# A linear attention layer in four overlapping passes: DMA order, three score banks, wider masks, and a norm placed behind the feature chain

## The chip, the cores and the metric

The kernel runs on one core of one Trainium2 chip. The metric is the device time of one execution in microseconds, lower is better. It is given as the median of several executions. One further execution was taken by the hardware profiler, and every row below is from that one.

The engines are PE (TensorE, matmuls; its weight loads are listed as PEld), DVE (VectorE), ACT (ScalarE), POOL (GpSimd) and SP (SyncE, which here only issues DMAs). Each runs its own instructions strictly in order; they meet only at semaphores.

## The reference, cut to what matters

The kernel computes two layers on 4 sequences of 512 tokens with 512 values each. A layer is half a feed-forward step, an attention, and half a feed-forward step again. The change lies in the first layer's attention, and in what is woven around it:

```python
x = x + 0.5 * _L0_ffn_ref(_layernorm(x), ...)        # routed splines, first half
x = x + _L0_attn_ref(_layernorm(x), ...)             # the attention below
x = x + 0.5 * _L0_ffn_ref(_layernorm(x), ...)        # routed splines, second half
# in _L0_attn_ref, with h = _layernorm(x):
def _softmax_kernel(x, R):
    n = sqrt(sum(x * x, -1));  x = x / maximum(n, 1e-06)
    p = einsum('...d,ed->...e', x, R)
    return concatenate([sin(p), cos(p)], -1) / sqrt(F)
q = rotary(h @ Wq.T + bq);  k = rotary(h @ Wk.T + bk)   # 16 query heads, 8 key heads
qp = _softmax_kernel(q, rand_matrix);  kp = _softmax_kernel(k, rand_matrix)
kv  = einsum('bhsf,bhsd->bsfd', kp, v)               # per token, over the heads
out = einsum('bhsf,bsfd->bhsd', qp, kv)
return out @ Wo.T + bo
```

The two sums run per token and over its heads, so no token sees another. The kernel puts 16 tokens side by side in one matmul (a group), computes all their scores, and multiplies by a mask that keeps each token's own.

## The kernel before, in words

**Passes.** The tokens come in four chunks of 512 (NCH = 4). `bass_macaron` calls `b_tensor`, `b_scalar`, `b_pool`, `b_sync` and `b_vector` for i = -1 to 3. Pass i works on four chunks at once (`b_roles`): the scores and outputs of chunk `now` = i; the projections and features of `new` = i + 1; the end of the first feed-forward half and the layer norm of `look` = i + 2; and the token routing of `back` = i - 1 for the second half. Chunks that do not exist are left out: pass -1 has no scores, passes 2 and 3 have no `look`, pass 3 has no `new`.

**Loop.** Each pass has a loop over y = 0 to 16. A pair y is two groups, 32 tokens. On PE `score(y)` makes the scores of a pair in a PSUM bank (L1310). On DVE `mask(y)` multiplies them by the constant mask into `sm` (L1688), which has two buffers. On PE `weighted(y)` multiplies by the values (L1323) into a bank of sums. After four pairs `sums(g)` reads that bank, on ACT (L1479), then on DVE (L1696). Between these stand the other chunks' steps at set values of y: twelve matmuls of 512 columns each for a projection (`project`, L1195, at y in QK_AT), its rotation on DVE (L1706) and POOL (L1595, L1599), the lengths (`length`, L1342), the values (`value`), and on DVE the routing steps (`route_pick_vector`, L517 and L519; `token_sums_vector`, L372 to L377; `route_ends_vector`, L527 to L539) and the look steps (`look_slope_vector` at y = 8; `scale_tiles_vector` at y = 12).

**Feature chain.** At y = 16 and behind the loop the lengths are spread (PE L1362, copied by ACT L1495) and six features follow (z = 0 and 1 of the keys, 2 to 5 of the two query pairs). Each is made by DVE (`angle`, L1730 to L1735), ACT (`feature`, L1501 and L1504, the high part) and DVE again (`low`, L1742, the low part). `ang` has two buffers, so feature z + 2 starts behind `low(z)`.

**Through DRAM.** The features are laid out anew by a trip through `feat_dram`. SP stores the high parts as they come and loads them back in another layout (`b_sync`), POOL does so with the low parts (`b_low_spread`). A load waits until the stores that it reads have landed. ACT copies the keys into `ksg` (`keys(g)`, L1512). `score(0)` of the next pass waits for all query loads, for `keys(0)`, and for `residual(3)`, which is the last step of this pass.

**End of a pass.** `output(u)` (L1195, twelve matmuls each for u = 0 to 3) makes the rows and `residual(u)` (L1750 on DVE) adds them to x. Two banks serve the four, so `output(2)` waits for `residual(0)` and `output(3)` for `residual(1)`. `residual(0)` stands behind `low(5)` on DVE. POOL then adds the bias (L1615). The layer norm of `look` takes the sums on DVE (L2108), two activations on ACT, `norm_refine_vector` on DVE, four activations that write the rows (L2150), sixteen transposes on PE, four for each column block (`next_turn_tensor`, L1933), and a split by ACT (L1941) and DVE (L1948). In passes 1 and 2 PE also runs the route steps (L447 to L479) of `back` before the next pass.

Of the kernel before, what the change touches and what calls it, by code (L numbers as in the profile page):

```python
# [1211 lines left out]
SCORE_BANK = (0, 1)  # L1212
SUM_BANK = (4, 5)
# [15 lines left out]
LOOK_SCALE, LOOK_NORM = 12, 16  # L1229
# [61 lines left out]
def b_tensor(k, pe, i):  # L1291
# [7 lines left out]
    def score(y):  # L1299
# [7 lines left out]
        need(pe, s["b_mask"], PAIRS * now + y - 1)  # L1307
        for q in range(2):
            toks = slice((2 * y + q) * GROUP, (2 * y + q + 1) * GROUP)
            ins = pe.matmul(k.ps[:, SCORE_BANK[y % 2], 256 * q:256 * q + 256].rearrange("p (h t) -> p h t", h=16),  # L1310
                            k.ksg[0:96, 2 * y + q, :], k.qs[0:96, :, toks], start=True, stop=True)
        ins.then_inc(s["b_s"], 1)

    def weighted(y):
        if y == 0:
            pe.wait_ge(s["b_vr"], 128 * (now + 1))
        if y % 4 == 0 and y >= 8:
            pe.wait_ge(s["b_ot_lo"], TPC * now + y // 4 - 1)
        pe.wait_ge(s["b_mask"], PAIRS * now + y + 1)
        for q in range(2):  # L1320
            g = 2 * y + q
            for j in range(4):
                ins = pe.matmul(k.ps[32 * j:32 * j + 32, SUM_BANK[y // 4 % 2], :]  # L1323
# [32 lines left out]
    def spread(a):  # L1356
        if a == 0:
            pe.wait_ge(s["b_r"], new + 1)
            if now is not None:
                pe.wait_ge(s["b_ot_lo"], TPC * now + 3)  # L1360
# [67 lines left out]
    if look is not None:  # L1428
# [42 lines left out]
def b_scalar(k, e, i):  # L1471
# [78 lines left out]
    ahead = look is not None and now is not None  # L1550
    if ahead:
        norm_root_scalar(k, e, look)
# [5 lines left out]
    if ahead:  # L1558
        next_rows(range(2))
    spread(2)  # L1560
    feature(2)
    if ahead:
        next_rows(range(2, TPC))
# [3 lines left out]
    if ahead:  # L1567
        next_turns(range(2))
    elif look is not None:
# [63 lines left out]
def b_low_spread(k, e, i):  # L1633
# [3 lines left out]
    for a in range(3):  # L1637
        for z in (2 * a, 2 * a + 1):
            e.wait_ge(s["b_f_lo"], 6 * i + z + 1)
            b_store(k, e, 1, z, s["b_lo_out"])  # L1640
        if a == 0:
            if i == 0:
                e.wait_ge(s["ug_out"], 16 * NCH)
            need(e, s["b_ksg"], 4 * i)
        if a == 1:
            need(e, s["b_s"], PAIRS * i)
        e.wait_ge(s["b_lo_out"], 96 * i + 32 * (a + 1))
        b_load(k, e, 1, a, 1 if a else 2, s["b_qs2" if a else "b_ks2"])


def b_sync(k, sp, i):
# [14 lines left out]
    for a in range(3):  # L1666
        for z in (2 * a, 2 * a + 1):
            sp.wait_ge(s["b_f_hi"], 6 * i + z + 1)
            b_store(k, sp, 0, z, s["b_hi_out"])
        if a == 0:  # L1670
            need(sp, s["b_ksg"], 4 * i)
        if a == 1:
            need(sp, s["b_s"], PAIRS * i)
        sp.wait_ge(s["b_hi_out"], 96 * i + 32 * (a + 1))
        for rows in ((0, 2) if a else (0, 1)):
            b_load(k, sp, 0, a, rows, s["b_qs" if a else "b_ks"])


def b_vector(k, V, i):
# [4 lines left out]
    def mask(y):  # L1684
        e.wait_ge(s["b_s"], PAIRS * now + y + 1)
        need(e, s["b_pv"], PAIRS * now + y - 1)
        for q in range(2):
            ins = e.tensor_tensor(k.sm[:, y % 2, q], k.ps[:, SCORE_BANK[y % 2], 256 * q:256 * q + 256]  # L1688
                                  .rearrange("p (h t) -> p h t", h=16), bcast(k.c["same"].unsqueeze(1), [P, 16, 16]),
                                  ALU.mult)  # L1690
        ins.then_inc(s["b_mask"], 1)

    def sums(g):
        e.wait_ge(s["b_ot_hi"], TPC * now + g + 1)
        out = grouped(k.ot_lo)[:, :, :, 8 * g:8 * g + 8]
        e.scalar_tensor_tensor(out=out, in0=k.ps[:, SUM_BANK[g % 2], :].rearrange("p (a h g) -> p a h g", g=8, a=4),  # L1696
# [73 lines left out]
    for y in range(PAIRS + 1):  # L1770
# [16 lines left out]
        if look is not None:  # L1787
# [14 lines left out]
            if y == LOOK_NORM and now is not None:  # L1802
# [1216 lines left out]
```

## Time and profile before

| what | value |
|---|---|
| median of 3 runs | 2215.35 us (2211.72 to 2221.18) |
| the profiled execution's own time | 2216.09 us |
| its span | 2214.3 us |
| PE busy | 1947.4 us, 88% of the span |
| DVE busy | 1254.1 us, 57% |
| ACT busy | 716.2 us, 32% |
| POOL busy | 275.5 us, 12% |

The span is the time between the first and the last instruction in the trace. An engine's busy time leaves out its waits. Below, times are microseconds from the start of the span. The passes with scores are found by the first `score(0)` of each: 311.45, 399.06, 493.16 and 578.61 us; the last outputs start at 620.57 us.

### The profile page before, as it was taken

The page shows a single profiled execution, that of the slowest core. Times are in us where ns is not written, and L with a number is a line of the kernel's source. Part 1 is how long each engine was busy: PE and PEld are TensorE (multiplying, and loading weights), DVE is VectorE, ACT ScalarE, POOL GpSimd, SP SyncE. Part 2 cuts the span into 40 slices and gives each one's busy share as a digit, 9 for nine tenths or more (in the row PEclk, how much of TensorE's full clock was granted, in tenths as well). Part 3 has the DMA queues.
Part 4 walks back from the last instruction along what each step waited for, and adds up shares of the span by engine and source line. Part 5 has one row for each costly group of instructions (what it writes and reads, how often), then busy time and mean ns, then how long its engine had stood idle before and what let it go on. Part 6 is the DMA issues. An engine that isn't in the chain of part 4 may idle for free.

```text
span 2214.3 us, 28789 instructions
## 1 busy us (share of the span) xinstructions
PE 1947.4 (88%) x11782; PEld 925.7 (42%) x11782; DVE 1254.1 (57%) x2297; ACT 716.2 (32%) x1105; POOL 275.5 (12%) x224
## 2 busy tenths in 40 slices
PE   3876768878655999899999999999999999999999
PEld 2443324434333444344444444444444444444444
DVE  4677568677765564636673456636663456533332
ACT  3553143253422123222352234422352234311211
POOL 1840234332100000000000100010000100000000
PEclk9987778979767999999999999999999999999999
DMA  7223242141323213211021111111021111132321
GB/s 242 93 84 88 110 91 56 36 91 18 74 77 115 96 64 117 95 67 40 28 77 40 65 48 58 48 58 44 25 77 36 70 48 58 48 114 100 120 98 64
DMA packets 92457, 164.93 MB, mean 74 GB/s; under 512 B 44134, under 2 KB 55718, under 8 KB 87718
## 3 DMA queue, kind: packets, MB, share of 16 engines
q1 hardware_dynamic: 89446, 156.79, 22.3%
q0 software_dynamic: 2880, 6.31, 1.1%
q8 instruction: 93, 1.52, 0.3%
q14 instruction: 38, 0.31, 0.0%
HBM read 137.89 MB, written 25.17 MB: 74 GB/s over the span
## 4 chain that ended last, share of the span: by engine, by line
PE 50%; DVE 4%; ACT 2%; issue 1%; ACTq 0%; DVEq 0%
PE ps L1195 27%; PE ps L2018 12%; PE ps L2532 2%; PE ps L2551 1%; DVE arena L2696 1%; PE ps L2528 1%; PE ps L2534 1%; PE ps L2478 1%; PE ps L2569 1%; PE ps L2553 1%; PE ps L2555 1%; PE ps L2560 1%; PE ps L2558 1%; PE ps L2475 1%; DVE arena L2073 0%
## 5 line engine op out<-in xcount | busy, mean ns | idle before, releaser
L1195 PE MATMUL ps<-arena 128*128 128x512 f16 (+1 forms) x4512 | 1015.6, 380 | 25.1 <-DVE arena L2073 12.9
L1195 PEld LDWEIGHTS ps<-arena 128*128 128x128 f16 x4512 | 433.2, 98 | 539.2 <-issue 42.4
L2018 PE MATMUL ps<-arena 128*128 128x512 f16 x1536 | 343.8, 379 | 12.5 <-DVE arena L2101 9.3
L2018 PEld LDWEIGHTS ps<-arena 128*128 128x128 f16 x1536 | 146.6, 97 | 185.8 <-DVE arena L2101 12.1
L2073 DVE SCALAR_TENSOR_TENSOR arena<-arena,ps 128x512 f32<-128x512 f32 x128 | 87.9, 687 | 208.4 <-ACT arena L2040 207.8
L2040 ACT ACTIVATE arena<-ps,arena 128x512 f32<-128x512 f32 x128 | 87.6, 684 | 358.7 <-PE ps L1195 358.5
L2625 ACT ACTIVATE arena<-ps 128x1024 f32<-128x1024 f32 (+3 forms) x128 | 90.1, 704 | 254.7 <-PE ps L2534 254.5
L2730 DVE CAST arena<-arena 128x1024 f16<-128x1024 f32 (+3 forms) x128 | 66.2, 517 | 150.3 <-ACT arena L2625 148.3
L2696 DVE TENSOR_REDUCE arena<-ps 128x2 f32<-128x256 f32 (+3 forms) x128 | 99.6, 820 | 65.0 <-PE ps L2478 65.0
L2101 DVE SCALAR_TENSOR_TENSOR arena<-ps,arena 128x512 f32<-128x512 f32 x64 | 44.0, 688 | 134.5 <-PE ps L2018 134.3
L2082 DVE SCALAR_TENSOR_TENSOR arena<-ps,arena 128x512 f32<-128x512 f32 x128 | 95.8, 748 | 39.5 <-PE ps L1195 39.1
L2676 POOL TENSOR_TENSOR arena<-arena 128x512 f16<-128x512 f32 x32 | 37.1, 1158 | 624.7 <-ACT arena L2603 624.7
L2732 DVE TENSOR_TENSOR arena<-arena 128x1024 f16<-128x1024 f32 (+3 forms) x128 | 111.4, 870 | 4.4
L2064 DVE TENSOR_TENSOR arena<-arena 128x512 f16<-128x512 f32 x128 | 90.9, 710 | 4.0 <-ACT arena L2032 4.0
L1933 PE MATMUL ps<-arena 128*128 128x128 f32 x192 | 32.9, 323 | 67.2 <-ACT arena L2150 64.7
L2680 POOL TENSOR_TENSOR arena<-arena 128x512 f32<-128x512 f32 x16 | 19.0, 1187 | 581.7 <-DVE arena L2743 581.7
L2032 ACT ACTIVATE arena<-arena 128x512 f16<-128x512 f32 x128 | 79.7, 622 | 17.5 <-DVE arena L2082 17.5
L741 PE MATMUL ps<-arena 128*128 128x128 f32 x240 | 46.9, 341 | 37.6 <-DVE arena L979 17.6
L2600 ACT ACTIVATE arena<-ps 128x512 f32<-128x512 f32 x32 | 19.1, 597 | 166.7 <-PE ps L1195 166.7
L2532 PE MATMUL ps<-arena 32*128 32x512 f16 (+3 forms) x768 | 72.9, 293 | 0.0
L1688 DVE TENSOR_TENSOR arena<-ps,arena 128x256 f32<-128x256 f32 x128 | 47.6, 417 | 41.8 <-PE ps L1310 41.1
L1323 PE MATMUL ps<-arena 128*32 128x64 f32 x1024 | 41.8, 292 | 26.3 <-DVE arena L1688 26.2
(269 smaller groups left out, 2356.6 us busy)
## 6 DMA issues: line engine op xcount, KB each, us to landing
arena<-wug_dram SPq DMA_DIRECT2D x128, 512.0 KB, 3.3
arena<-wd_hi_dram SPq DMA_DIRECT2D x16, 1024.0 KB, 5.0
arena<-wd_lo_dram SPq DMA_DIRECT2D x16, 1024.0 KB, 7.1
wug_dram<-arena SPq DMA_DIRECT2D x4, 2048.0 KB, 16.5
arena<-feat_dram SPq DMA_DIRECT2D x24, 256.0 KB, 3.9
arena<-_attn_hidden_states_dram SPq DMA_DIRECT2D x4, 1024.0 KB, 16.9
arena<-in_L_ffn_W_up_dram SPq DMA_DIRECT2D x8, 512.0 KB
arena<-in_L_ffn_W_down_dram SPq DMA_DIRECT2D x4, 1024.0 KB, 7.3
```

The costliest lines, as they stand in the source:

```text
L1195: ins = pe.matmul(out, left[a](c), right[b](c), start=(at == 0), stop=(at == 3 * n - 1))
L2018: ins = pe.matmul(k.ps[:, bank, :], act[x][:, slot, cols], wd[y][:, f, :], start=(f == 0 and m == 0), stop=(f == 7 and m == 2))
L2032: e.activation(k.act_hi[:, g % ACT_SLOTS, :], k.prod[:, g % 2, :], ACT.Copy).then_inc(s["f_hi"], 1)
L2040: e.activation(k.th[:, g % 2, :], k.ps[:, GATE_BANK, :], ACT.Tanh, scale=k.wscale[:, FB + a:FB + a + 1])\
L2064: e.tensor_tensor(k.act_lo[:, g % ACT_SLOTS, :], k.prod[:, g % 2, :], k.act_hi[:, g % ACT_SLOTS, :], ALU.subtract)\
L2073: e.scalar_tensor_tensor(out=th, in0=th, scalar=1.0, in1=k.ps[:, GATE_BANK, :], op0=ALU.add, op1=ALU.mult)\
L2082: e.scalar_tensor_tensor(out=k.prod[:, g % 2, :], in0=k.ps[:, UP_HALF_BANK, :], scalar=k.wscale[:, a:a + 1], in1=th, op0=ALU.mult, op1=ALU ...
L2532: pe.matmul(k.ps[:, bank, queries], x[rows, 4 + b, keys], y[rows, b, queries], start=False, stop=False)
L2625: e.activation(k.p32[:, t % 2, :, queries], k.ps[:, 0:2, queries], ACT.Exp, scale=SCORE).then_inc(s["c_exp"], 1)
L2696: e.tensor_reduce(k.mx[:, u, 4 * b + 2 * j:4 * b + 2 * j + 2], k.ps[:, bank:bank + 2, 0:(u + 1) * P], AXX, ALU.max).then_inc(s["c_max"], 1)
L2730: e.tensor_copy(k.p_hi[:, t % 2, :, queries], k.p32[:, t % 2, :, queries]).then_inc(s["c_p_hi"], 1)
L2732: e.tensor_tensor(k.p_lo[:, t % 2, :, queries], k.p32[:, t % 2, :, queries], k.p_hi[:, t % 2, :, queries], ALU.subtract).then_inc(s["c_p_l ...
```

## The change

There are three edits in one.

1. Features. Both queues store the four query features (z = 2 to 5) first, wait once for all, and then load both query pairs. Before, the first pair was loaded ahead of the second pair's stores.
2. Scores. `SCORE_BANK` has three banks instead of two and `SUM_BANK` one instead of two. PE issues `score(y + 1)` at loop step y, ahead of `weighted(y - 1)`, so scores run one more pair ahead. With one bank of sums, `weighted(4)`, `weighted(8)` and `weighted(12)` wait until DVE has read the sums of the four pairs before. A mask is one DVE instruction of 512 columns instead of two of 256.
3. Norm of `look`. Where a pass has both `now` and `look` (passes 0 and 1), its sums, roots and rows move from the end of the loop and from between the features to behind `low(5)` and `residual(0)`. On PE the four transposes move behind `output(2)`. On ACT they come ahead of `keys(0)`, as before.

```diff
-SCORE_BANK = (0, 1)
-SUM_BANK = (4, 5)
+SCORE_BANK = (0, 1, 4)
+SUM_BANK = 5
...
 def b_tensor(k, pe, i):
...
-        need(pe, s["b_mask"], PAIRS * now + y - 1)
+        need(pe, s["b_mask"], PAIRS * now + y - 2)
...
-        if y % 4 == 0 and y >= 8:
-            pe.wait_ge(s["b_ot_lo"], TPC * now + y // 4 - 1)
+        if y % 4 == 0 and y:
+            pe.wait_ge(s["b_ot_lo"], TPC * now + y // 4)
...
-            if y < PAIRS:
-                score(y)
-            elif new is not None:
+            if y == 0:
+                score(0)
+            if y + 1 < PAIRS:
+                score(y + 1)
+            if y == PAIRS and new is not None:
                 spread(0)
...
-        next_turn_tensor(k, pe, look, 0)
-        next_turn_tensor(k, pe, look, 1)
     output(0)
     output(1)
+    output(2)
     if look is not None:
-        next_turn_tensor(k, pe, look, 2)
-        next_turn_tensor(k, pe, look, 3)
-    output(2)
+        for c in range(KC):
+            next_turn_tensor(k, pe, look, c)
...
 def b_vector(k, V, i):
...
-        for q in range(2):
-            ins = e.tensor_tensor(k.sm[:, y % 2, q], k.ps[:, SCORE_BANK[y % 2], 256 * q:256 * q + 256]
-                                  .rearrange("p (h t) -> p h t", h=16), bcast(k.c["same"].unsqueeze(1), [P, 16, 16]),
-                                  ALU.mult)
+        ins = e.tensor_tensor(k.sm[:, y % 2].rearrange("p q h t -> p (q h) t"),
+                              k.ps[:, SCORE_BANK[y % 3], :].rearrange("p (h t) -> p h t", t=16),
+                              bcast(k.c["same"].unsqueeze(1), [P, 32, 16]), ALU.mult)
...
-            if y == LOOK_NORM and now is not None:
-                next_sums()
...
-    if look is not None and now is not None:
-        norm_refine_vector(k, V, look)
...
-    if look is not None and now is None:
+    residual(0)
+    if look is not None:
         next_sums()
         norm_refine_vector(k, V, look)
-    residual(0)
-    turned(0)
     residual(1)
-    turned(1)
-    turned(2)
-    turned(3)
     residual(2)
+    for c in range(KC):
+        turned(c)
     residual(3)
```

The queue of SP is the first place. These are its DMAs of one chunk: the values out and in, then the features out (`feat_dram<-arena`) and in. Before:

```order
L1659 DMA values_dram<-arena 128x4x256
L1663 DMA arena<-values_dram 16x32x32 x8
L1622 DMA feat_dram<-arena 8x16x512 x2
L1629 DMA arena<-feat_dram 32x8x512 x2
L1622 DMA feat_dram<-arena 8x16x512 x2
L1629 DMA arena<-feat_dram 32x8x512 x2
L1622 DMA feat_dram<-arena 8x16x512 x2
L1629 DMA arena<-feat_dram 32x8x512 x2
```

and of the change:

```order
L1653 DMA values_dram<-arena 128x4x256
L1657 DMA arena<-values_dram 16x32x32 x8
L1613 DMA feat_dram<-arena 8x16x512 x2
L1620 DMA arena<-feat_dram 32x8x512 x2
L1613 DMA feat_dram<-arena 8x16x512 x4
L1620 DMA arena<-feat_dram 32x8x512 x4
```

The last pair's two stores have moved past the first pair's two loads. (Lines of the change are lower by three to nine numbers, as its file is shorter.)

The second place is PE from the last steps of pass 0 to the first of pass 1. L1362 is `spread`, L1352 `turned`, L1933 (L1924) the transposes of the next rows, L1195 the outputs and then a projection. Before:

```order
L1362 MATMUL ps<-arena 128x512
L1352 MATMUL ps<-arena 128x512 x2
L1362 MATMUL ps<-arena 128x512
L1933 MATMUL ps<-arena 128x128 x8
L1195 MATMUL ps<-arena 128x512 x24
L1933 MATMUL ps<-arena 128x128 x8
L1195 MATMUL ps<-arena 128x512 x24
L1310 MATMUL ps<-arena 128x256 x2
L1195 MATMUL ps<-arena 128x512 x12
L1310 MATMUL ps<-arena 128x256 x2
L1323 MATMUL ps<-arena 32x64 x8
```

and of the change:

```order
L1362 MATMUL ps<-arena 128x512
L1352 MATMUL ps<-arena 128x512 x2
L1362 MATMUL ps<-arena 128x512
L1195 MATMUL ps<-arena 128x512 x36
L1924 MATMUL ps<-arena 128x128 x16
L1195 MATMUL ps<-arena 128x512 x12
L1310 MATMUL ps<-arena 128x256 x4
L1195 MATMUL ps<-arena 128x512 x12
L1310 MATMUL ps<-arena 128x256 x2
L1323 MATMUL ps<-arena 32x64 x8
```

Three outputs now stand ahead of all sixteen transposes and one behind them, and two pairs of scores ahead of the first projection.

The third place is DVE at the end of pass 0 in the change, from `low(3)` on. L2099 to L2109 are the sums of the next rows (before they were L2108 to L2118, ahead of `angle(0)`), L1747 is `residual`, L1939 the split of the transposed rows:

```order
L1739 SCALAR_TENSOR_TENSOR arena<-arena 128x512 x2
L1747 SCALAR_TENSOR_TENSOR arena<-ps,arena 128x512
L2099 BN_STATS arena<-arena 128x6 x4
L2107 BN_AGGR arena<-arena 128x2 x4
L2109 TENSOR_SCALAR arena<-arena 128x4
L2127 TENSOR_TENSOR arena<-arena 128x4
L2128 SCALAR_TENSOR_TENSOR arena<-arena 128x4
L2129 SCALAR_TENSOR_TENSOR arena<-arena 128x4
L2130 TENSOR_SCALAR arena<-arena 128x4
L2131 SCALAR_TENSOR_TENSOR arena<-arena 128x4
L1747 SCALAR_TENSOR_TENSOR arena<-ps,arena 128x512 x2
L1939 TENSOR_TENSOR arena<-ps,arena 128x512 x4
```

`residual(1)` and `residual(2)` now stand behind the norm, and `residual(3)` behind all four splits.

## Rows read from the trace of the kernel before

**Rows 1.** Windows: length; busy PE, PEld, DVE, ACT, POOL; PE clock, DMA share, GB/s.

```profile
579.00:620.00 41.00, 22.99 (x335) 13.44 (x333) 33.19 (x83) 9.52 (x17) 0.00 (x0) 0.62 0.01 2
...
694.00:2214.00 1520.00, 1471.60 (x8709) 666.95 (x8707) 780.22 (x1299) 464.23 (x723) 75.70 (x64) 1.00 0.20 67
```

**Rows 2.** Waits of PE from 311 to 621: us in total, times, longest.

```profile
PE ps L1323 <- DVE arena L1688: 26.2, 13, 4.2
```

**Rows 3.** Timeline: masks and weighted sums, passes 1 and 2; start, duration, instruction [idle before].

```profile
413.85 0.65 PE L1323 MATMUL ps<-arena 128*32 128x64 f32 x16 [1.56 <-DVE arena L1688]
414.44 2.77 PE L1195 MATMUL ps<-arena 128*128 128x512 f16 x12
...
498.90 0.76 DVE L1688 TENSOR_TENSOR arena<-ps,arena 128x256 f32<-128x256 f32 x2 [4.34 <-PE ps L1310]
...
510.69 0.65 PE L1323 MATMUL ps<-arena 128*32 128x64 f32 x16 [3.71 <-DVE arena L1688]
511.27 4.45 PE L1195 MATMUL ps<-arena 128*128 128x512 f16 x12
```

**Rows 4.** Timeline: PE and DVE around the sums of pass 0.

```profile
344.63 0.65 PE L1323 MATMUL ps<-arena 128*32 128x64 f32 x16
...
346.17 0.69 DVE L1696 SCALAR_TENSOR_TENSOR arena<-ps,arena 128x512 f16<-128x512 f32 x1
...
360.89 0.66 PE L1323 MATMUL ps<-arena 128*32 128x64 f32 x16 [2.84 <-DVE arena L1688]
```

**Rows 5.** Timeline: last query loads of pass 0 and first scores of pass 1.

```profile
395.41 0.60 POOL L1629 DMA_DIRECT2D arena<-feat_dram  x1 [4.66 <-DMA feat_dram<-arena]
...
399.06 0.41 PE L1310 MATMUL ps<-arena 96*128 96x256 f16 x2 [2.68 <-issue]
399.28 4.44 PE L1195 MATMUL ps<-arena 128*128 128x512 f16 x12
```

**Rows 6.** Timeline: the norm of pass -1, which has no scores.

```profile
299.12 2.87 DVE L2108 BATCH_NORM_STATS2 arena<-arena 128x6 f32<-128x512 f32 x4
...
307.19 1.94 PE L1933 MATMUL ps<-arena 128*128 128x128 f32 x8 [16.34 <-ACT arena L2150]
309.69 1.97 PE L1933 MATMUL ps<-arena 128*128 128x128 f32 x8 [0.56 <-DVE arena L1948]
```

**Rows 7.** Timeline: start and end of the feature chains in passes 0, 1 and 2.

```profile
368.95 0.60 ACT L1495 ACTIVATE arena<-ps 128x512 f32<-128x512 f32 x1 [10.17 <-PE ps L1362]
...
384.82 0.69 DVE L1742 SCALAR_TENSOR_TENSOR arena<-arena 128x512 f16<-128x512 f32 x1 [0.85 <-ACT arena L1504]
...
457.10 0.60 ACT L1495 ACTIVATE arena<-ps 128x512 f32<-128x512 f32 x1 [9.91 <-PE ps L1362]
...
473.20 0.69 DVE L1742 SCALAR_TENSOR_TENSOR arena<-arena 128x512 f16<-128x512 f32 x1 [0.85 <-ACT arena L1504]
...
548.64 0.69 DVE L1730 SCALAR_TENSOR_TENSOR arena<-ps,arena 128x512 f32<-128x512 f32 x1 [3.47 <-ACT arena L1495]
...
562.10 0.69 DVE L1742 SCALAR_TENSOR_TENSOR arena<-arena 128x512 f16<-128x512 f32 x1 [0.85 <-ACT arena L1504]
```

**Rows 8.** Timeline of PE: from the route steps of pass 1 to pass 2.

```profile
482.19 1.04 PE L447 MATMUL ps<-arena 128*128 128x128 f32 x8
483.06 2.75 PE L1195 MATMUL ps<-arena 128*128 128x512 f16 x12
...
493.16 0.61 PE L1310 MATMUL ps<-arena 96*128 96x256 f16 x2
```

**Rows 9.** Timeline: the end of pass 2 and two waits of pass 3.

```profile
574.28 4.22 POOL L1615 TENSOR_TENSOR arena<-arena 128x512 f32<-128x512 f32 x4
575.62 3.45 DVE L517 TENSOR_TENSOR arena<-arena 128x512 f32<-128x512 f32 x1
...
580.09 0.68 DVE L517 TENSOR_TENSOR arena<-arena 128x512 f32<-128x512 f32 x1
...
612.67 0.76 DVE L1688 TENSOR_TENSOR arena<-ps,arena 128x256 f32<-128x256 f32 x2 [1.26 <-PE ps L1310]
```

More of the change, by code:

```diff
@@ L1228 @@
 LOOK_START, LOOK_PLACE, LOOK_SLOPE, LOOK_VALUE = 3, 6, 8, 11
-LOOK_SCALE, LOOK_NORM = 12, 16
+LOOK_SCALE = 12
 def need(eng, sem, value):
@@ L1359, in spread @@
             if now is not None:
-                pe.wait_ge(s["b_ot_lo"], TPC * now + 3)
+                pe.wait_ge(s["b_mask"], PAIRS * (now + 1))
         need(pe, s["b_spread"], 3 * new + a)
@@ L1548, in next_turns @@
             turn_scalar(k, e, look, c, NEXT_TURN[c])
-    ahead = look is not None and now is not None
-    if ahead:
-        norm_root_scalar(k, e, look)
     if now is None:
@@ L1557, in b_scalar @@
     feature(1)
-    if ahead:
-        next_rows(range(2))
     spread(2)
     feature(2)
-    if ahead:
-        next_rows(range(2, TPC))
     feature(3)
@@ L1566, in b_scalar @@
     feature(5)
-    if ahead:
-        next_turns(range(2))
-    elif look is not None:
+    if look is not None:
         use_log(e)
@@ L1636, in b_low_spread @@
     need(e, s["b_qs2"], 32 * i)
[L1637 to L1648, printed above, removed]
+    for z in range(2):
+        e.wait_ge(s["b_f_lo"], 6 * i + z + 1)
+        b_store(k, e, 1, z, s["b_lo_out"])
+    if i == 0:
+        e.wait_ge(s["ug_out"], 16 * NCH)
+    need(e, s["b_ksg"], 4 * i)
+    e.wait_ge(s["b_lo_out"], 96 * i + 32)
+    b_load(k, e, 1, 0, 2, s["b_ks2"])
+    for z in range(2, 6):
+        e.wait_ge(s["b_f_lo"], 6 * i + z + 1)
+        b_store(k, e, 1, z, s["b_lo_out"])
+    need(e, s["b_s"], PAIRS * i)
+    e.wait_ge(s["b_lo_out"], 96 * i + 96)
+    for a in (1, 2):
+        b_load(k, e, 1, a, 1, s["b_qs2"])
 def b_sync(k, sp, i):
@@ L1665, in b_sync @@
     need(sp, s["b_qs"], 64 * i)
[L1666 to L1676, printed above, removed]
+    for z in range(2):
+        sp.wait_ge(s["b_f_hi"], 6 * i + z + 1)
+        b_store(k, sp, 0, z, s["b_hi_out"])
+    need(sp, s["b_ksg"], 4 * i)
+    sp.wait_ge(s["b_hi_out"], 96 * i + 32)
+    for rows in (0, 1):
+        b_load(k, sp, 0, 0, rows, s["b_ks"])
+    for z in range(2, 6):
+        sp.wait_ge(s["b_f_hi"], 6 * i + z + 1)
+        b_store(k, sp, 0, z, s["b_hi_out"])
+    need(sp, s["b_s"], PAIRS * i)
+    sp.wait_ge(s["b_hi_out"], 96 * i + 96)
+    for a in (1, 2):
+        for rows in (0, 2):
+            b_load(k, sp, 0, a, rows, s["b_qs"])
 def b_vector(k, V, i):
@@ L1695, in sums @@
         out = grouped(k.ot_lo)[:, :, :, 8 * g:8 * g + 8]
-        e.scalar_tensor_tensor(out=out, in0=k.ps[:, SUM_BANK[g % 2], :].rearrange("p (a h g) -> p a h g", g=8, a=4),
+        e.scalar_tensor_tensor(out=out, in0=k.ps[:, SUM_BANK, :].rearrange("p (a h g) -> p a h g", g=8, a=4),
                                scalar=O_SCALE, in1=grouped(k.ot_hi)[:, :, :, 8 * g:8 * g + 8],
@@ L1841, in b_vector @@
     low(5)
-    if look is not None and now is None:
+    residual(0)
+    if look is not None:
         next_sums()
         norm_refine_vector(k, V, look)
-    residual(0)
-    turned(0)
     residual(1)
-    turned(1)
-    turned(2)
-    turned(3)
     residual(2)
+    for c in range(KC):
+        turned(c)
     residual(3)
```

6 lines of the change are left out of this document (3 added, 3 removed).

## The prediction, made before the changed kernel ran

> **What bounds the kernel now.** I read the windows first. From 694 us on PE is busy for 1471.6 of 1520 us at full clock [rows 1]; the change touches none of that, it only moves it in time. So what counts is when the four passes end. In pass 3 PE works 23.0 us of 41 and DVE 33.2 us [rows 1]: there DVE sets the pace. In passes 0 to 2 PE is mostly busy but stands at joints. The waits of PE name the largest: 26.2 us in 13 waits of the weighted sums for a mask [rows 2]. That looks like the prize for a third score bank, so I asked of each wait what DVE did before it. In pass 2 it first stood 4.34 us without scores and was late afterwards [rows 3]. In pass 0, before the wait of 2.84 us at 360.89 [rows 4], it worked through the look steps: there more scores help little.
>
> The second joint is the start of a pass. `score(0)` of pass 1 waits 2.68 us after the outputs; POOL's last query load was issued at 395.41 [rows 5]. So the trip through DRAM is the bound there. At the start of pass 2 PE comes straight from its route steps [rows 8], and the loads are hidden.
>
> **The change, part by part.** All shifts are against the time before; minus is earlier.
>
> *Stores ahead of loads.* It takes a load's time out of the way of POOL's last stores, worth 2.68 us at 399.06 at most, and nothing at the other starts. Whether it pays depends on what else is late then, which is the norm, next.
>
> *The norm behind the features.* Take pass 2 as the price of a feature chain without the norm: 548.64 to 562.79 (562.10 + 0.69), 14.15 us [rows 7]. In pass 0 the copy that the chain waits for ends at 369.55; I put it 0.3 us later (below) and add 0.1 for the hop: `low(5)` ends at 369.95 + 14.15 = 384.1, before at 385.51 [rows 7]. That is the gain, 1.4 us. What now hangs behind it is in pass -1, where the norm also stands behind the features: from the first sum at 299.12 to the end of the last transpose at 311.66 (309.69 + 1.97), 12.54 us [rows 6]. Then come `output(3)` and `residual(3)`, which must be done before `score(0)`:
>
> 384.1 + 0.69 (`residual(0)`) + 12.54 = 397.3 for the last transpose; + 4.44 for twelve matmuls at the low clock, since PE has idled (as at 399.28 after 2.68 us [rows 5]) = 401.8; + 0.8 for `residual(3)` and its hop = 402.6.
>
> Before it was 399.06 [rows 5]: 3.5 us later, and by then the loads, which were in by 399.06 before and now go out earlier, have landed. Part comes back: `project(0)` follows PE's own work and runs its twelve in 2.77 as at 414.44 [rows 3] instead of 4.44 (-1.7), while one more pair of scores stands ahead of it (+0.3). First joint: **+2.1 us**.
>
> Second joint, in times of pass 1 before. The copy ends at 457.70 [rows 7]; with the loop's -1.1 (below) `low(5)` ends at 457.7 - 1.1 + 0.1 + 14.15 = 470.85, before at 473.89. Then + 0.69 + 12.54 = 484.1 for the last transpose. The route steps wait for its split too. That takes 1.5 us: the second row of transposes began at 309.69, and its split block was ready at about 308.2, half of the first row [rows 6]. So the route steps start at 485.6 instead of 482.19, +3.4. `output(3)` before took 2.75 [rows 8]; PE has now idled for several us ahead of the transposes, so I take 4.44, +1.7. Behind it the chain to 493.16 is as it was. Second joint: **+5.1 us**, the gain of the chain included.
>
> *Scores ahead, three banks.* In pass 2 DVE's idle 4.34 us before 498.90 now take in that mask and the first route pick, some 2.4 us (mask 0.7, pick 1.7: the tensor op and its reduction, of which the first is 0.68 elsewhere); the extra pair on PE costs 0.3. The mask that PE waits for at 510.69 [rows 3] comes 2.1 us earlier, and that shift runs down DVE's and POOL's chain to the end of the pass. PE alone could gain more, as a wait of 1.56 us left the next twelve at 2.77 and one of 3.71 at 4.45 [rows 3], but the next wait for sums eats it. Pass 2: **-2.1 us**.
>
> *One bank of sums.* `weighted(8)` ran at 344.63 and must now wait for the sums of the first half, which DVE finished at 346.86 (346.17 + 0.69) [rows 4]: 2.3 us on PE. DVE is not earlier there, because its look step waits for a PE step that does not move. Of this, most is slack: PE later waited 2.84 us for the mask at 360.89 [rows 4], and that wait shrinks. The look step that sets it is itself some 0.3 us later. So pass 0 ends +0.3. In pass 1 the same chain gains since two masks no longer stand ahead of look steps, waiting for scores: -1.1 at the copy. Both numbers are already in the two joints.
>
> *Wide masks.* Two of 256 columns take 0.76 [rows 3]; one instruction of 512 columns out of PSUM takes 0.69 [rows 4]. 64 masks save 4.5 us of DVE, on its path only in the DVE-bound half of pass 3, six to nine masks: 0.4 us. The Trainium skill (VectorE: DVE Perf Modes, the section on the TRN2 errata) puts a PSUM-source instruction at 120 cycles plus one per column; by its figure at 0.96 GHz two of 256 would be 0.78 us and one of 512 0.66, an estimate that would make the saving 0.12 instead of 0.07 and the term 0.7. The trace has both times, so they stand.
>
> *Pass 3.* At 575.62 a DVE multiply that takes 0.68 took 3.45, while POOL's bias adds ran (574.28 to 578.50) [rows 9]. POOL stood in its queue behind the last loads. With the stores ahead it is spared one such round; in pass 0 POOL's wait for landed stores took 4.66 us [rows 5]. The adds then end at about 573.8, before 575.62. So -2.77, and DVE is busy without a gap from there to the first mask and on. Later a mask waited 1.26 us for scores [rows 9] that are now there. With the masks: **-4.4 us**. The Trainium skill (SBUF — State Buffer, Who interferes with whom) says that a DVE instruction with two SBUF inputs contends with a GpSimd instruction that reads SBUF. By it the 3.45 is contention and goes with the overlap; the row agrees.
>
> **Sum.** +2.1 + 5.1 - 2.1 - 4.4 = +0.7 us. Against the profiled execution's 2216.09 that is 2216.8; the median before is 0.7 below that execution, so I forecast **2216 us**: no change that could be told. A measurement of this kernel tells about 0.5%, 11 us, from no change.
>
> **Bounds.** Down: `output(3)` at the full clock at both joints (-3.4), pass 2 also keeps PE's faster projection (-1.7), pass 3 saves all its later waits (-1): -5.4 in sum. Up: pass 2 gains nothing (+2.1); POOL still overlaps and pass 3 gains 1.6 only (+2.8); the wait for sums of 2.3 us stays on the path in passes 0 and 1 (+4.6): +10.2 in sum. That is 2210 to 2226.
>
> **Rivals.**
>
> *It does what it says* (0.12): the mask waits go, and the norm hides behind the loads. For it: 26.2 us of waits [rows 2], 2.68 us at the loads [rows 5]. Against it: in passes 0 and 1 DVE was at work before its late masks, and the norm's 12.5 us are longer than the trip of the last pair. With both joints at zero instead of +7.2, the 2.7 us gained, and half of the 26.2, of which 3.4 are counted already (2.1 in pass 2, 1.3 in pass 3): 0.7 - 7.2 - 2.7 - 13.1 + 3.4 = -18.9, about 2197.
>
> *The bank of sums decides* (0.08), the other side. Three groups in each of four passes now make PE wait for ACT and DVE: 12 waits. One was worked out at 2.3 us [rows 4]. If no later slack takes them in, since each also costs PE its clock, they are 12 x 2.3 = 28 us, and the time 2240. From about 0.9 us a wait kept on the path it passes 11 us and decides. Against it: ahead of `weighted(4)` PE has a projection of 2.77 us to run in passes 0 to 2, longer than the two reads of a bank by ACT and DVE (0.69 on DVE [rows 4], about as much on ACT), and DVE's pace, not PE's, sets pass 3.
>
> *The clock.* PE's granted clock in pass 3 was 0.62 [rows 1], a mix of its two levels, 1.2 and 2.4 GHz; the low one cost 1.7 us for twelve matmuls after one wait of 3.71 us and nothing after one of 1.56 [rows 3]. If the new waits fall so that PE drops once more in each of the four passes, that is +6.8 us, still no change by the bound. Its chance, 0.1, is part of the forecast's 0.80. The Trainium skill (TensorE: Matmul & The Clock Gate, HAM oscillation) says that waits between bursts throttle PE again; the two rows agree.
>
> **How the numbers follow.** Forecast 0.80, between 2210 and 2226 but for a run's scatter of 4 us; 0.12 for the faster rival, 0.08 for the slower. So faster by over 0.5% 0.12, within 0.80, slower 0.08. The range is the forecast's own with that scatter downwards: 2207 to 2225. The rivals lie outside it.
>
> **What would show it.** Of each step: `score(0)` of pass 1 some 3.5 us after where it was, with `output(3)` and not a load before it, and the loads landed; between the first transposes and the end of `residual(0)` some 8 us on PE with little work. In pass 1 the route steps 15 us behind `low(5)` or more. A wait of `weighted(8)` for the sums of about 2.3 us in pass 0, and a shorter one than 2.84 at the thirteenth mask. L517 at 0.68 throughout in pass 3, POOL's adds done by then. A mask in one instruction of 0.69. The forecast is wrong if the transposes start less than 7 us behind `residual(0)`, if the passes' first halves shift by more than 2 us, or if anything behind 694 us changes its length.

## The result, and the profile after

The changed kernel takes 2218.86 us (median of 20 runs, 2214.70 to 2226.37), the kernel before 2214.25 us in the same comparison: ratio 1.0026, 95% interval 1.0017 to 1.0036. That is 4.6 us more, within the 0.5% that I called no change, and 2.9 us above the forecast. The profiled execution has a span of 2218.1 us.

First the waits of PE from 311 to 626 us (total, times, longest), against [rows 2]:

```profile
PE ps L1323 <- DVE arena L1693: 14.4, 7, 3.4
PE ps L1195 <- DVE arena L1747: 10.4, 3, 4.6
PE ps L1323 <- DVE arena L1685: 9.4, 7, 4.1
```

The waits for masks (L1685) fell from 26.2 to 9.4 us. In their place stand seven waits for the sums (L1693) of the one bank, 14.4 us, and outputs now wait 10.4 us for residuals, where before one waited 4.6 us. PE's timeline shows the two waits for sums in pass 0, and then the two joints, against [rows 4], [rows 5] and [rows 8]:

```profile
347.31 0.65 PE L1323 MATMUL ps<-arena 128*32 128x64 f32 x16 [2.08 <-DVE arena L1693]
...
362.45 0.65 PE L1323 MATMUL ps<-arena 128*32 128x64 f32 x16 [1.94 <-DVE arena L1693]
...
385.64 4.45 PE L1195 MATMUL ps<-arena 128*128 128x512 f16 x12 [3.74 <-DVE arena L1747]
393.47 1.97 PE L1924 MATMUL ps<-arena 128*128 128x128 f32 x8 [3.38 <-ACT arena L2141]
395.99 1.97 PE L1924 MATMUL ps<-arena 128*128 128x128 f32 x8 [0.56 <-DVE arena L1939]
397.76 3.62 PE L1195 MATMUL ps<-arena 128*128 128x512 f16 x12
402.16 0.61 PE L1310 MATMUL ps<-arena 96*128 96x256 f16 x4 [0.79 <-DVE arena L1747]
402.61 2.76 PE L1195 MATMUL ps<-arena 128*128 128x512 f16 x12
...
487.34 1.97 PE L447 MATMUL ps<-arena 128*128 128x128 f32 x8 [1.41 <-DVE arena L1939]
489.10 4.02 PE L1195 MATMUL ps<-arena 128*128 128x512 f16 x12
...
500.50 1.04 PE L1310 MATMUL ps<-arena 96*128 96x256 f16 x4
```

The reader is to see the chain of the norm in the second half of pass 0: residual(0), transposes at 393.47, `output(3)`, `residual(3)`, `score(0)` at 402.16. What I had not foreseen is on POOL. Its timeline in pass 0, and the end of pass 2, against [rows 9]:

```profile
381.26 0.61 POOL L1620 DMA_DIRECT2D arena<-feat_dram  x1 [2.75 <-DMA feat_dram<-arena]
381.86 1.19 POOL L1613 DMA_DIRECT2D feat_dram<-arena  x2
386.29 0.60 POOL L1613 DMA_DIRECT2D feat_dram<-arena  x1 [3.24 <-issue]
390.55 0.61 POOL L1613 DMA_DIRECT2D feat_dram<-arena  x1 [3.66 <-issue]
396.88 1.19 POOL L1620 DMA_DIRECT2D arena<-feat_dram  x2 [5.72 <-DMA feat_dram<-arena]
...
578.69 1.19 POOL L1620 DMA_DIRECT2D arena<-feat_dram  x2 [5.01 <-DMA feat_dram<-arena]
579.89 4.24 POOL L1606 TENSOR_TENSOR arena<-arena 128x512 f32<-128x512 f32 x4
```

and DVE's multiply there, then one wide mask:

```profile
581.45 3.24 DVE L517 TENSOR_TENSOR arena<-arena 128x512 f32<-128x512 f32 x1
...
507.42 0.68 DVE L1685 TENSOR_TENSOR arena<-ps,arena 128x512 f32<-128x512 f32 x1
```

The third and fourth query store wait 3.24 and 3.66 us "for issue". Of the first, 0.4 us is the wait for its own low part (ready at 383.44); nothing in the program holds the rest. The last low part was ready at 384.98 (384.29 + 0.69), its store went out at 390.55. So POOL's loads left at 396.88, later than the 395.41 of [rows 5], and the adds still ran beside L517, which took 3.24 us, against 3.45 before. SP, with the same order, issued its four stores from 381.28 to 384.85; only the fourth stood back, by 1.2 us, as its high part was ready at 384.25.

To compare executions, which differ by some us before the first pass, I count from POOL's first feature store in pass -1 (at 289.57 us before, 289.40 after). All in us, each line from the one profiled execution of its kernel; "rest" runs from the start of the last outputs to the end of the span:

| kernel | first store to pass 0 | pass 0 | pass 1 | pass 2 | pass 3 | rest |
|---|---|---|---|---|---|---|
| before | 21.9 | 87.6 | 94.1 | 85.5 | 42.0 | 1593.7 |
| changed | 23.6 | 89.2 | 98.3 | 84.1 | 40.9 | 1592.6 |
| changed, again | 24.1 | 89.6 | 97.5 | 83.7 | 40.6 | 1592.8 |
| edit 1 alone | 24.6 | 88.7 | 94.0 | 85.9 | 44.0 | 1598.5 |
| edit 2 alone | 22.7 | 87.4 | 91.8 | 82.8 | 41.1 | 1599.5 |
| edit 3 alone | 22.6 | 89.8 | 98.8 | 85.1 | 43.2 | 1592.7 |
| without edit 1 | 21.9 | 90.5 | 95.6 | 83.6 | 40.7 | 1592.6 |
| without edit 2 | 24.8 | 87.4 | 98.7 | 85.2 | 44.1 | 1598.8 |
| without edit 3 | 24.3 | 91.8 | 94.3 | 84.3 | 40.4 | 1593.3 |
| changed, low parts by SP | 23.1 | 89.2 | 96.0 | 82.3 | 40.3 | 1593.9 |
| changed, adds first | 24.3 | 89.6 | 98.3 | 84.0 | 39.7 | 1593.8 |
| before, low parts by SP | 21.9 | 87.9 | 93.6 | 85.3 | 38.8 | 1593.9 |
| edit 2, low parts by SP | 22.1 | 88.9 | 92.4 | 84.3 | 39.7 | 1593.8 |

### The profile page after: what moved, and what is told of

Same layout as the page of the kernel before. It is cut to its first block, busy times and chain, and to the rows that moved or that the text cites. A ratio compares the mean times of both kernels' runs of the same rounds, so it can differ in the third digit from the quotient of the medians.

```text
span 2218.1 us, 28723 instructions
## 1 busy us (share of the span) xinstructions
PE 1951.7 (88%) x11782; PEld 927.4 (42%) x11782; DVE 1251.9 (56%) x2233; ACT 709.8 (32%) x1099; POOL 276.2 (12%) x224
## 4 chain that ended last, share of the span: by engine, by line
PE 50%; DVE 4%; ACT 2%; issue 1%; ACTq 0%; DVEq 0%
PE ps L1195 27%; PE ps L2009 12%; PE ps L2523 2%; PE ps L2542 1%; DVE arena L2687 1%; PE ps L2519 1%; PE ps L2525 1%; PE ps L2469 1%; PE ps L2560 1%; PE ps L2544 1%; PE ps L2546 1%; PE ps L2551 1%; PE ps L2549 1%; PE ps L2466 1%; DVE arena L2064 0%
## 5 line engine op out<-in xcount | busy, mean ns | idle before, releaser
L1195 PE MATMUL ps<-arena 128*128 128x512 f16 (+1 forms) x4512 | 1017.0, 380 | 30.1 <-DVE arena L2064 12.9
L1195 PEld LDWEIGHTS ps<-arena 128*128 128x128 f16 x4512 | 433.4, 98 | 546.9 <-issue 45.8
L2009 PE MATMUL ps<-arena 128*128 128x512 f16 x1536 | 343.8, 379 | 12.5 <-DVE arena L2092 9.3
L2064 DVE SCALAR_TENSOR_TENSOR arena<-arena,ps 128x512 f32<-128x512 f32 x128 | 87.9, 687 | 208.4 <-ACT arena L2031 207.8
L1924 PE MATMUL ps<-arena 128*128 128x128 f32 x192 | 34.4, 336 | 65.1 <-ACT arena L2141 63.4
L784 PE MATMUL ps<-arena 128*128 128x512 f16 x256 | 63.1, 390 | 0.9 <-DVE arena L979 0.9
L1323 PE MATMUL ps<-arena 128*32 128x64 f32 x1024 | 41.7, 293 | 23.9 <-DVE arena L1693 14.4
```

Source lines behind the costliest of these rows:

```text
L1195: ins = pe.matmul(out, left[a](c), right[b](c), start=(at == 0), stop=(at == 3 * n - 1))
L2009: ins = pe.matmul(k.ps[:, bank, :], act[x][:, slot, cols], wd[y][:, f, :], start=(f == 0 and m == 0), stop=(f == 7 and m == 2))
L2064: e.scalar_tensor_tensor(out=th, in0=th, scalar=1.0, in1=k.ps[:, GATE_BANK, :], op0=ALU.add, op1=ALU.mult)\
```

## The experiments

My theory after the result (A): the norm makes the two joints late, as predicted, and POOL's queue takes only a few transfers that have not landed, so edit 1 makes POOL's loads later instead of earlier. The rivals: the order of the DMAs hides behind the norm (B); the bank of sums makes the loss.

**The edits undone one at a time.** Edit 1 undone is the two functions `b_low_spread` and `b_sync` as before, edit 3 undone the removed lines of the diff put back. In short:

```diff
 # dma_order_back
+    for a in range(3):
+        for z in (2 * a, 2 * a + 1): ... b_store(k, e, 1, z, s["b_lo_out"])
+        ... b_load(k, e, 1, a, 1 if a else 2, s["b_qs2" if a else "b_ks2"])
 # norm_back
+            if y == LOOK_NORM and now is not None:
+                next_sums()
 # banks_back
-SCORE_BANK = (0, 1, 4)
-SUM_BANK = 5
+SCORE_BANK = (0, 1)
+SUM_BANK = (4, 5)
```

> The changed kernel with the DMA order of before in both queues (the first query pair is loaded ahead of the second pair's stores). Theory A, POOL's queue holds only two or three transfers, so that its third and fourth store wait to be issued: no store waits any more, the last POOL load of pass 0 goes out at about 395.4 + 1 instead of 396.88, score(0) of pass 0 comes 1.5 us earlier (311.5), the adds of pass 2 end before L517, which falls from 3.24 to 0.68, and pass 3 is 2.6 us shorter: in sum 3 to 4 us less than the changed kernel. Theory B, the order of the DMAs is hidden behind the norm: score(0) of passes 1 to 3 and the time stay within 1 us of the changed kernel. Both: the start of pass 1 is set by output(3) and stays at 402.

> The changed kernel with the norm of look in its old place. Theory A (the norm behind residual(0) is what makes the joints late, but POOL's late loads stand right behind it): pass 1 starts with a wait for POOL's loads at about 401.5 instead of 402.2, so the first joint gives back under 1 us; the second joint, where PE has the route steps, gives back 3 to 5 us, and the time falls by 3 to 5 us. Theory B, the prediction's joints as they stand (2.1 and 5.1): it falls by 7. If it does not fall at all, the lateness of the joints is from the sum bank instead.

> The changed kernel with edit 2 undone (two score banks, two banks of sums, narrow masks), so edits 1 and 3 alone. If these two make the loss, as theory A has it (the norm's place and POOL's full queue), it stays 4 to 7 us slower than before, and the start of pass 1 relative to the first feature store of pass -1 is again near 112.5. If the bank of sums made the loss, it is back at the time of before.

Without edit 1: 2215.26 against 2212.49 us before, ratio 1.0013 (0.9999 to 1.0027). No store waits for issue any more and pass 0 starts at 21.9 again, but the adds still ran beside L517, which took 3.02 us; that part of the expectation failed. Pass 1 starts where it did, counted from the first store (112.4 against 112.8), as both said. The loss of 2.8 us stands against 4.6 and 5.5 in the two comparisons of the changed kernel, so undoing edit 1 gives back 2 to 3 us, less than the 3 to 4 of A and more than the 1 of B.

Without edit 3: 2220.77 against 2212.49, 1.0024 (1.0010 to 1.0038). It did not fall. PE's waits say why: pass 1 now begins with a wait of 6.08 us for the loads, which POOL issued at 400.34 and 400.94. Partly the norm had hidden them: in the changed kernel the second load landed at 401.7, 0.4 us ahead of the end of `residual(3)`. Partly they are later: counted from the first store, the last low part is ready at 98.9 instead of 95.6, as the norm's steps stand among the features again, and the loads leave at 111.2 instead of 107.5. Edit 2 alone has that late end too (98.1 against 95.9 before). The expectation of 3 to 5 us gained failed for these reasons.

Without edit 2: 2227.89 against 2213.74, 1.0050 (1.0033 to 1.0066). So the bank of sums did not make the loss; without it the kernel is 8.6 us slower than the changed one in the same comparison (2219.28, next).

**Each edit alone, and the changed kernel again.**

> The kernel before with edit 1 alone (all query stores ahead of the query loads, in both queues). If POOL's full queue is what edit 1 costs (seen in the runs with and without it), POOL's last load of pass 0 goes out 1 to 3 us later than in the kernel before, the waits of score(0) at the starts of passes 0 and 1 grow, L517 stays long in pass 3, and it is 4 to 8 us slower than before. The prediction's account had it neutral to 2.7 us faster at the start of pass 1 and 2.77 faster in pass 3.

> The kernel before with edit 3 alone (the norm of the next rows behind residual(0)). The prediction's joints: +2.1 and +5.1, so 7 us slower than before, with output(3) and residual(3) ahead of score(0) of pass 1 and no wait for loads. From the two runs with edit 2 that differ in it alone (2212.7 without, 2215.3 with) it is 3 to 4 us.

> The kernel before with edit 2 alone: three score banks, one bank of sums, wide masks. The prediction's terms: pass 2 and pass 3 gain 2.1 and 1.7, passes 0 and 1 lose 0.3 and gain 1.1, so 3 to 4.5 us faster than before. Rival, the bank of sums decides: seven waits of 14.4 us in sum for the sums take the place of the mask waits (26.2 down to about 9) and the time is that of before or up to 3 us slower.

> The changed kernel itself once more, as the measure for the other runs of this call and for its own spread. Theory: the 2.4 us by which pass 1 was longer in its first profile than in the profiles of two kernels that do the same there (98.34 against 95.62 and 95.99) is the granted clock of one execution, not the change; then in this profile output(3) of pass 1 takes 2.75 instead of 4.02 and L447 1.09 instead of 1.97, or again the long times if it belongs to the kernel. Median 2216 to 2219.

Edit 1 alone costs most of all: 2226.35 against 2214.14, 1.0054 (1.0037 to 1.0071). POOL, PE and DVE in its timeline:

```profile
385.82 0.60 POOL L1622 DMA_DIRECT2D feat_dram<-arena  x1 [1.96 <-issue]
389.13 0.60 POOL L1622 DMA_DIRECT2D feat_dram<-arena  x1 [2.71 <-issue]
396.48 1.19 POOL L1629 DMA_DIRECT2D arena<-feat_dram  x2 [6.75 <-DMA feat_dram<-arena]
...
401.29 0.58 PE L1310 MATMUL ps<-arena 96*128 96x256 f16 x2 [6.04 <-issue]
...
577.51 4.59 DVE L517 TENSOR_TENSOR arena<-arena 128x512 f32<-128x512 f32 x1
```

The wait at the start of pass 1, which the edit was to remove (2.68 us in [rows 5]), is 6.04 us, and the multiply beside the adds went from 3.45 to 4.59. Of the 9.3 us by which this profile's span is longer, 4.8 lie in the rest.

Edit 3 alone: 2223.43 against 2214.14, 1.0039 (1.0025 to 1.0053). In the table pass 0 is 2.2 us longer and pass 1 4.7. These are not the prediction's 2.1 and 5.1, which are counted between other points: from first score to first score its terms for this edit make 3.2 (3.5 less 0.3 for the one bank) and 4.5 (5.1 - 1.7 for `project(0)` + 1.1 that edit 2 was to gain), 7.7 in sum for a measured 6.9. The first scores of pass 1 wait for `residual(3)`, not for a load:

```profile
403.54 0.38 PE L1310 MATMUL ps<-arena 96*128 96x256 f16 x2 [0.85 <-DVE arena L1739]
```

Edit 2 alone: 2212.71 against 2213.74, 0.9990 (0.9975 to 1.0006). In its profile the four passes take 6.0 us less than before (303.1 against 309.1), but the rest takes 5.7 us more. Two stretches that differ, 60 to 80 and 280 to 320 us behind the start of the last outputs; before, then edit 2 alone (columns as in [rows 1]; the clock is the third number from the end):

```profile
680.57:700.57 20.00, 10.54 (x48) 6.39 (x49) 8.40 (x21) 7.70 (x12) 0.00 (x0) 0.69 0.03 5
900.57:920.57 20.00, 15.36 (x67) 6.46 (x66) 16.85 (x23) 4.84 (x6) 0.00 (x0) 0.94 0.42 163
920.57:940.57 20.00, 18.55 (x84) 8.06 (x83) 13.84 (x25) 10.55 (x16) 0.00 (x0) 0.98 0.25 80
```

```profile
674.04:694.04 20.00, 9.60 (x36) 5.68 (x37) 8.58 (x20) 7.70 (x12) 0.00 (x0) 0.56 0.02 3
894.04:914.04 20.00, 15.82 (x73) 6.86 (x71) 15.86 (x22) 4.90 (x6) 0.00 (x0) 0.99 0.52 184
914.04:934.04 20.00, 18.10 (x70) 7.46 (x71) 14.06 (x26) 9.19 (x14) 0.00 (x0) 0.84 0.17 53
```

PE's clock was low for longer in both stretches. In the second stretch the two windows have to be taken together: 3.2 us of 40 at 1.2 GHz before and 6.8 with edit 2 alone, and 3.6 us more at half speed are 1.8 us of work at most. A third place lies 520 to 540 us behind the last outputs, with a granted share of 1.00 before and 0.91 now. The starts of the same DVE instructions in both traces, counted from the last outputs, show what each place costs: edit 2 alone is 0.9 us late already 20 us behind them (its last outputs took 13.41 us against 12.48), 2.6 behind the first place, 3.9 behind the second and 5.6 behind the third. So work that the change does not touch gave the gain back in this execution. Edit 1 alone and the kernel without edit 2 have a rest of 1598.5 and 1598.8 and lose at the same three places. Why these three kernels and not the others stays open; each has one profile, and the times of one kernel spread by up to 12 us (edit 2 alone: 2206.53 to 2218.37), so it is not shown that all their executions do so.

The changed kernel again: 2219.28 against 2213.74, 1.0018 (1.0004 to 1.0033). Pass 1 took 97.5 us, its `output(3)` 3.48 and its first route step L447 1.97; so my theory that the long pass 1 was one execution's clock holds only in part: 0.8 us of it. Where both ran at the full clock (1.09 and 2.75, without edit 1 and with the low parts by SP, below), pass 1 took 95.6 and 96.0. And in this second profile it was a load, not `residual(3)`, that pass 1 waited for:

```profile
403.47 0.60 PE L1310 MATMUL ps<-arena 96*128 96x256 f16 x4 [1.90 <-issue]
```

`residual(3)` was done at 402.29. POOL's fourth query store had waited 4.47 us, its second load left at 399.17 and landed 4.1 us later. So the full queue of edit 1 costs 1.2 us at this joint in one of two profiles of the changed kernel.

**The two costs of edit 1 by themselves.**

```diff
 # low_by_sp: in b_sync, and z = 4, 5 left out in b_low_spread
         b_store(k, sp, 0, z, s["b_hi_out"])
+        if z > 3:
+            sp.wait_ge(s["b_f_lo"], 6 * i + z + 1)
+            b_store(k, sp, 1, z, s["b_hi_out"])
 # low_by_sp: in b_low_spread, ahead of the two loads
+    e.wait_ge(s["b_hi_out"], 128 * i + 128)     # all of SP's stores
 # adds_first: in b_low_spread, pass 2 only
+    ahead()      # the four bias adds
     for a in (1, 2):
         b_load(k, e, 1, a, 1, s["b_qs2"])
 # small_ring
-dynamic_dma_scratch_size=1024
+dynamic_dma_scratch_size=512
```

> The changed kernel, but the low parts of the last two features are stored by SP's queue instead of POOL's. Theory A (POOL's queue is full): POOL's loads no longer follow two stalled stores, the last load of pass 0 goes out at about 391 instead of 396.9, score(0) of pass 0 at 310 to 311.5 instead of 313.0, L517 in pass 3 falls from 3.24 to 0.68: 3 to 5 us less in all. Rival (POOL's issue waits only mirror busy DMA engines): SP's stores of the low parts land as late, POOL's loads go out within 1 us of before, and the time is unchanged. The start of pass 1 stays at 401 to 402, set by the norm.

> The changed kernel, with POOL's four bias adds of pass 2 ahead of its last two query loads instead of behind. If contention of these adds with the DVE multiply L517 costs 2.6 us at the start of pass 3's second half, L517 takes 0.68 throughout and the last outputs start some 2.5 us earlier (623.0), while the loads go out at 578.7 as now. Rival: DVE has slack there, L517 gets short but the time stays (under 0.5 us).

> The changed kernel with the on-chip memory for the descriptors of POOL's DMAs halved, from 1024 to 512. Theory A (a POOL store waits to be issued because the descriptors of earlier transfers, not yet landed, fill this memory): the issue waits appear already at the second store or load and grow, POOL's loads go out several us later, and each start of a pass with them, 5 to 20 us in all. Rival (DVE's work keeps POOL from writing descriptors, or the DMA engines are full): the issue waits of 3 to 4 us at the third and fourth store stay as they are.

Low parts by SP: 2217.43 against 2212.49, 1.0020 (1.0006 to 1.0034). POOL's last loads left at 390.30 and 390.90, six us earlier, and L517 took 0.69; the profiled span fell by 4.6 us to 2213.5, but the medians show no gain: 4.9 us above the kernel before, where the changed kernel was 4.6 and 5.5. The start of pass 1 stayed with `residual(3)`.

Adds first: 2216.47 against 2212.49, 1.0011 (0.9997 to 1.0025). L517 took 0.69, and the first mask of pass 3 came 0.6 us behind the first scores (581.15, 581.79) instead of 2.8 (584.60, 587.41). But pass 3 is only 1.0 to 1.3 us shorter than in the two profiles of the changed kernel, not 2.5: the rest went to later waits, which I did not follow one by one.

Small ring: 2248.84 us (2 runs) against 2214.14, 1.0156 (1.0125 to 1.0187). POOL in its pass 0, and PE's first scores of pass 1:

```profile
388.72 0.61 POOL L1613 DMA_DIRECT2D feat_dram<-arena  x1 [3.78 <-DVE arena L1739]
392.84 0.60 POOL L1620 DMA_DIRECT2D arena<-feat_dram  x1 [3.51 <-DMA feat_dram<-arena]
396.89 0.60 POOL L1613 DMA_DIRECT2D feat_dram<-arena  x1 [3.45 <-issue]
401.21 0.60 POOL L1613 DMA_DIRECT2D feat_dram<-arena  x1 [3.71 <-issue]
...
411.90 0.61 POOL L1620 DMA_DIRECT2D arena<-feat_dram  x1 [2.89 <-DMA feat_dram<-arena]
415.42 0.60 POOL L1620 DMA_DIRECT2D arena<-feat_dram  x1 [2.91 <-issue]
...
419.17 1.01 PE L1310 MATMUL ps<-arena 96*128 96x256 f16 x4 [9.20 <-issue]
```

With half the memory for descriptors the waits begin at the second key store (388.72, its low part was ready at 386.02), and each later transfer goes out only when the one before it has landed, mostly some 0.3 us behind it. That costs about 30 us against the changed kernel, more than the 5 to 20 expected. DVE's work was not changed and the transfers were the same, so the rival falls and theory A stands, that this memory is what holds POOL. A larger memory was not tried.

**Versions that use it.**

```diff
 # before_lows_by_sp (norm, banks as before): SP as in low_by_sp, one mask of 512 columns; POOL:
+    b_load(k, e, 1, 1, 1, s["b_qs2"])           # behind the stores of z = 2, 3
+    e.wait_ge(s["b_hi_out"], 128 * i + 128)     # all of SP's stores
+    b_load(k, e, 1, 2, 1, s["b_qs2"])
 # lows_by_sp_and_banks: the same queues, and edit 2
```

> The kernel before with two edits: SP's queue puts all its stores ahead of its loads and also stores the low parts of the last two features, so that POOL's last load stands behind landed stores only; and masks in one instruction of 512 columns. Norm and banks as before. Theory A: POOL's last load of pass 0 goes out at about 391 instead of 395.41, the wait of 2.68 us at the start of pass 1 is gone, the adds of pass 2 are done ahead of L517 (3.45 to 0.68), masks save 0.4: in sum 5 to 6 us faster than before. Rival: PE has another wait right behind each (residual(3), a later mask), and only 1 to 2 us are gained.

> Edit 2 (banks, wide masks) together with SP's queue storing the low parts of the last two features, norm in its old place: the two versions that came out 1 us below before each. If their gains add (the one at the starts of passes and in L517, the other in passes 1 and 2), it is 3 to 6 us faster than before; if both only shift work to the next wait, 0 to 2.

The first: 2212.44 against 2213.74, 0.9988 (0.9974 to 1.0003). L517 took 0.69 and pass 3 38.8 us, but PE's wait at the start of pass 1 stayed, 3.05 us. POOL's last load left at 390.02, but SP's four, all behind its stores now, take from 389.66 to 392.71 to issue; the last one started at 392.26 and landed 6.0 us later, at 398.2, and the scores start at 398.31. The rival was right here. The second: 2211.61 against 2214.14, 0.9985 (0.9971 to 0.9999), the only one whose interval lies below the kernel before, and by 0.0001 only: a gain of 2.5 us is likely, not certain, with this many versions compared. Its first scores of pass 1 still wait:

```profile
397.35 0.60 PE L1310 MATMUL ps<-arena 96*128 96x256 f16 x4 [3.22 <-DMA arena<-feat_dram]
```

## Why the prediction was right, and where it was not

Its verdict and range held; some of its terms did not. Point by point, with the starts of the passes as a ruler (times of the changed kernel's first profile; the forecast ones are the prediction's sums):

- **The joints** were right in mechanism, and the first one's clock time with some luck. `score(0)` of pass 1 was forecast for 402.6 and came at 402.16; that of pass 2 for 500.4 (493.16 + 2.1 + 5.1), and came at 500.50. Transposes, `output(3)` and `residual(3)` stand in the order worked out, with `project(0)` at 2.76. But pass 0 itself grew by 1.6 us (89.2 against 87.6), not by the 3.5 that 402.6 stands for; the other 1.5 us came in with a late start of pass 0, which the forecast had at nothing. From that start the feature chain ended 0.65 us earlier than worked out (72.0 against 72.65 us) and `output(3)` took 3.62 instead of 4.44. And in the second profile the loads, not `residual(3)`, ended this wait, which the prediction had ruled out. Edit 3 alone gives 2.2 and 4.7 us for 3.2 and 4.5: the second size holds, the first was too large by a third. The second joint's size hangs on PE's clock there, low in most of these kernels as assumed, full in two. The route steps were forecast for 487.7 (485.6 in times of pass 1 before, and the first joint's 2.1) and came at 487.34, `output(3)` took 4.02 for 4.44.
- **The bank of sums** was right in kind: `weighted(8)` waited 2.08 us where 2.3 were forecast. The sum had no term for `weighted(12)`, 1.94 us. Seven waits instead of twelve appeared, and mask waits shrank by 16.8 us against 14.4. It does not decide: edit 2 alone is no loss.
- **Pass 2** gained 1.35 us instead of 2.1; edit 2 alone gained 2.7 there. The mask of the fourth pair is waited for 1.21 us at 515.38 instead of 3.71, and the projection behind it runs at 2.77 as hoped, but waits for sums of 1.64 and 1.35 us follow.
- **The step that failed** is "With the stores ahead it is spared one such round", and with it "the loads, which [...] now go out earlier". POOL is spared a round of waiting for landed stores, and gets two waits for issue instead, 3.24 and 3.66 us. So the adds of pass 2 began at 579.89, L517 kept 3.24 us, and pass 3 gained 1.0 us instead of 4.4. The same mistake made pass 0 start later, 1.5 us at 312.98 against 311.45, where I had counted nothing; without edit 1 it starts at 21.9 behind the first store, as before. Of the 4.3 us by which the last outputs came later than forecast (625.54 against 620.57 + 0.7), 3.4 are pass 3's.
- The contention itself was read rightly: the Trainium skill (SBUF — State Buffer, Who interferes with whom) says that a DVE instruction with two SBUF inputs contends with a GpSimd instruction that reads SBUF. The traces agree and show more. In each of the four runs where the adds ended ahead of L517 it took 0.69 us; in the nine where it started among them it ended 0.55 to 0.57 us behind the last add, whenever it had started (before: adds to 578.50, L517 to 579.07; changed: 584.13 and 584.69), while the adds kept their 1.06 us each. So the multiply waits out the whole row of adds, and its 3.45 us only say how early in that row it began. The 2.77 came through with the banks as before (38.8 against 42.0 us in pass 3, masks of 0.4 included) and only in part with edit 2 (0.3 to 1.4 us), so beside edit 2 the term was too large even with L517 short.
- **The rival "does what it says"** fell mainly for the reason given: at the second joint, and at the first by 0.4 us in one profile, the norm is longer than the loads' trip. The clock, which I had as +6.8 in the passes, moved time outside them too, in three of the other kernels.

The edits do not add up: alone they cost +12.2, -1.0 and +9.3 us (medians less those of before), together +4.6. One reason is shown. Edits 1 and 3 both delay the start of pass 1, one by the loads and one by the norm, and PE waits only for the later: counted from the first store it starts at 113.3 with edit 1 alone, 112.4 with edit 3 alone and 112.2 with both (before 109.5). This holds with the old banks only: edits 1 and 2 together, without edit 3, start it at 116.1, where edit 2 alone starts it at 110.1. The other is the rest of 1598.5 to 1599.5 us, which three of the eight combinations have; what sets it is open.

## What to carry to other kernels

Before moving a queue's stores ahead of its loads, count how many transfers will then be under way at once on that queue, and ask whether it can hold them; "waits for issue" on a row of DMAs is the sign that it cannot. Two things that delay the same start can cost only the larger, so measure each alone before keeping either, and also in pairs: edit 1 moved the start of pass 1 by 3.8 us alone, by 6.0 beside edit 2 and by 0.4 beside edits 2 and 3. And judge a gain of a few us by the whole program's median: in the profile of edit 2 alone, stretches up to 540 us behind the last outputs gave back 5.7 of 6.0 us.

## What the runs showed of the hardware that was not expected

POOL's DMA queue took no further store of 128 KB while one load of 256 KB and two stores were still under way. The third query store went out 0.3 us after that load had landed (386.29 and 385.98), and the fourth 0.3 us after the third had landed (390.55 and 390.2), although the two stores between had landed by 386.8 and 388.0. The other profiles with edit 1 and four query stores on POOL (changed again, edit 1 alone, without edit 2, without edit 3, adds first) show the same two steps. So it is not a plain count of transfers; what exactly holds the room is not shown. With half the descriptor memory each transfer goes out only behind the landing of the one before, and the kernel is 34.7 us slower than the kernel before. SP issued four such stores in 3.57 us without a wait for landings. The Trainium skill (DMA: Bandwidth & Descriptors, SWDGE vs HWDGE vs iDMA) says that the software path of GpSimd appends its descriptors to rings in SBUF, and that DMAs issued from SP never touch this path; the runs agree as far as halving that memory changed POOL's issues. SP is not free of delays either: with the low parts' stores on its queue one of its load issues took 1.67 us instead of 0.45.

The DVE multiply L517, both inputs in SBUF, ended 0.55 to 0.57 us behind the last of a row of GpSimd bias adds among which it had started, in the nine runs where this happened at the start of pass 3 and once more in the small-ring run (516.83, 4.57 us). Beside the longer GpSimd instructions L696 it was let in between two of them (before: start 79.78, 2.78 us, the next L696 began at 82.09), so this is shown for the adds alone, and why they differ is open.

The granted clock can rise later far behind a change, for one and the same code: with edit 2 alone the granted share was 0.91 against 0.96 before over 40 us some 300 us behind the last outputs, and 0.91 against 1.00 some 520 us behind them, each in one execution.
